# Attention over a normalised image: the exchange of flipped blocks sent through DRAM, and half of the value products in three short passes

## The reference

```python
y = group_norm(x, 4 groups) * gamma + beta           # per batch
q, k, v = split(einsum('bchw,dc->bdhw', y, w_qkv) + b_qkv)
scores = einsum('bnc,bcm->bnm', q, k) * C ** (-0.5)  # 1024 x 1024 per batch
w = softmax(scores)
a = einsum('bnm,bmc->bnc', w, v)
out = einsum('bchw,dc->bdhw', a, w_out) + b_out
return x + out
```

## Time and profile before

| | us |
|---|---|
| median of 3 runs | 137.71 (137.03 to 138.33) |
| profiled execution, device time | 138.07 |
| profiled execution, span of its instructions | 136.3 |
| PE busy | 129.4 (95%) |
| DVE busy | 99.8 (73%) |
| ACT busy | 65.0 (48%) |
| POOL busy | 41.4 (30%) |
| DMA traffic | 19.01 MB, queue q1 (SP) 53.8% of 16 engines' span |

### The profile page before, as it was taken

How to read it: one execution, slowest core, us unless ns; L and a number is a source line. 1 busy time by engine, 2 the same in 40 slices (tenths; PEclk the granted TensorE clock), 3 DMA queues, 4 the chain that set the end, 5 groups by cost and what they waited for, 6 DMA issues and landing times.

```text
span 136.3 us, 1759 instructions
## 1 busy us (share of the span) xinstructions
PE 129.4 (95%) x543; PEld 89.1 (65%) x543; DVE 99.8 (73%) x170; ACT 65.0 (48%) x117; POOL 41.4 (30%) x49
## 2 busy tenths in 40 slices
PE   6999999998999949999999999999999999999990
PEld 6987688875777526666666666666656577554670
DVE  0589699999998996877686889866868886761302
ACT  3154778854675372544542475544633474730000
POOL 6032130730022229300190058000770367303210
PEclk9999999999999999999999999999999999999999
DMA  4940000030056978985689656888888459961011
GB/s 152 350 191 0 0 5 0 3 77 0 0 111 147 210 188 236 207 203 169 154 204 206 204 114 160 191 195 224 203 202 201 122 123 209 209 176 77 0 77 77
DMA packets 8937, 19.01 MB, mean 139 GB/s; under 512 B 3040, under 2 KB 3040, under 8 KB 8928
## 3 DMA queue, kind: packets, MB, share of 16 engines
q1 hardware_dynamic: 8640, 18.63, 53.8%
q10 hardware_dynamic: 288, 0.27, 0.6%
HBM read 4.20 MB, written 2.11 MB: 46 GB/s over the span
## 4 chain that ended last, share of the span: by engine, by line
PE 75%; DVE 12%; SPq 7%; issue 2%; DMA 2%; DVEq 0%
PE mixed L833 31%; PE scores L778 7%; SPq L255 7%; PE scores L779 7%; PE scores L781 7%; DVE scores L577 5%; PE scores L839 4%; PE turned L798 3%; DVE flipped_odd L605 3%; PE turned L723 3%; DMA home_odd<-flipped_odd 2%; PE mixed L830 1%; PE mixed L828 1%; PE mixed L829 1%; PE mixed L723 1%
## 5 line engine op out<-in xcount | busy, mean ns | idle before, releaser
L577 DVE TENSOR_SCALAR_CACHE_REDUCE scores<-scores,key_bias 128x1024 f32<-128x1024 f32 x31 | 40.0, 1289 | 15.0 <-PE scores L781 14.7
L426 ACT ACTIVATE probs<-scores,neg_max 128x1024 f32<-128x1024 f32 x32 | 35.7, 1116 | 22.7 <-DVE scores L577 21.9
L833 PE MATMUL mixed<-home_odd,v 128*128 128x512 f32 x48 | 22.6, 594 | 1.9 <-DMA home_odd<-flipped_odd 1.9
L833 PE MATMUL mixed<-home_even,v 128*128 128x512 f32 x48 | 22.1, 594 | 0.0
L778 PE MATMUL scores<-y_hi_odd,z_hi_odd 128*128 128x512 f32 x32 | 18.7, 585 | 0.6 <-DVE z_lo_odd L544 0.6
L778 PE MATMUL scores<-y_hi_even,z_hi_even 128*128 128x512 f32 x30 | 15.9, 531 | 0.0
L605 DVE STREAM_TRANSPOSE flipped_odd<-probs 128x1024 f32<-128x1024 f32 x12 | 14.8, 1235 | 0.3 <-DMA home_odd<-flipped_odd 0.3
L605 DVE STREAM_TRANSPOSE flipped_even<-probs 128x1024 f32<-128x1024 f32 x12 | 14.8, 1234 | 0.0
L833 PEld LDWEIGHTS mixed<-home_even,v 128*128 128x128 f32 x48 | 8.9, 189 | 7.8 <-issue 7.2
L833 PEld LDWEIGHTS mixed<-home_odd,v 128*128 128x128 f32 x48 | 8.5, 190 | 8.3 <-issue 8.0
L779 PE MATMUL scores<-y_lo_odd,z_hi_odd 128*128 128x512 f32 x32 | 12.6, 392 | 0.0
(11 more groups left out here) (162 smaller groups left out, 202.9 us busy)
## 6 DMA issues: line engine op xcount, KB each, us to landing
home_odd<-flipped_odd SPq DMA_DIRECT2D x48, 128.0 KB, 2.4
home_even<-flipped_even SPq DMA_DIRECT2D x48, 128.0 KB, 2.4
out_dram<-result SPq DMA_DIRECT2D x8, 256.0 KB, 3.5
inv_wide<-inverse_rows SPq DMA_DIRECT2D x7, 256.0 KB, 3.6
xs<-in_x_dram SPq DMA_DIRECT2D x2, 512.0 KB, 6.5
xs<-in_x_dram SPq DMA_DIRECT2D x3, 256.0 KB, 4.6
xs<-in_x_dram ACTq DMA_DIRECT2D x1, 256.0 KB, 3.3
ws<-in_weights_dram SPq DMA_DIRECT2D x1, 256.0 KB, 4.0
```

The lines of the kernel that those rows point to most:

```text
L426: act.activation(probs[:, i % RING, :], scores[:, i % 2, :], ACT.Exp, bias=neg_max[:, i:i + 1], scale=-1.0, accum_out=row_sum[:, i:i + 1]) ...
L577: dve.tensor_scalar(scores[:, i % 2, :], scores[:, i % 2, :], key_bias[:, b % 2, i:i + 1], None, ALU.subtract, ALU.min, accum_out=neg_max[ ...
L833: mm = pe.matmul(bank, v[:, b % 2, k, :], there, start=first, stop=final)
```

## The change

The sixteen DMAs from SBUF to SBUF per group become four DMAs to a DRAM buffer `squares` (`keep`, one per block, 512 KB) and eight DMAs back (`bring`, two calls of four, each DMA 256 KB to 32 partitions). `bring(g, half)` waits until both kept blocks of its half have landed. `home` has three buffers, `flipped` is a ring of four tiles. `flip(n)` now waits until the pair of blocks with n-4 has landed in DRAM. SP's order for group g is `keep(4g)`, `keep(4g+1)`, `bring(g,0)`, `keep(4g+2)`, `keep_rows(g)`, `keep(4g+3)`, `bring(g,1)`, `spread_rows(g)`, and `store(g-2)` at the end as before. `add_residual(k)` moves from POOL's slot 4k+12 to slot 4k+14.

The eight key tiles of a group are four pairs. In groups 1 to 5 pairs 2 and 3, in group 6 pairs 1, 2 and 3, 13 pairs in all, are parted: ACT copies the head (`pair_head`, 128 x 1024), POOL subtracts to get the tail in place (`pair_tail`; the very last one on DVE), and PE takes three fp32r products per tile. The product with the tail comes a slot after those with the head. For that every batch's v is split: ACT copies `v_hi` as well as `v`, POOL makes `v_lo` (`value_tail`) in each batch. In POOL's slot n, `pair_tail` comes first, then `value_tail` (slots i = 2), and `add_residual` behind them.

`y` of batches 2 and 3 is made in slots 8 and 11 (before: 9 and 17), its head in slots 9 and 14, its tail in slots 9, 10 and 14, 15. The group statistics of batches 2 and 3 go to jobs V0 and V1 of slots 5 and 6 (before: V1 and V2 of slots 6 and 8).

```diff
-            def swap(group):
-                sp.wait_ge(s_flipped, QB * group)
-                if group > 2:
-                    sp.wait_ge(s_mixed, KT * (group - 1))
-                for k in range(SQ):
-                    for g in (0, 2, 1, 3):
-                        t = g ^ k
-                        sp.dma_start(home[group % 2][32 * t:32 * t + 32, g * N:(g + 1) * N],
-                                     flipped[group % 2][32 * g:32 * g + 32, t * N:(t + 1) * N]
-                                     ).then_inc(s_swapped[group % 2], 16)
+            def keep(n):
+                group, u = n // QB, n % QB
+                sp.wait_ge(s_flipped, n - QB + 1)
+                sp.dma_start(squares[group - 1, u // 2, :, :, u % 2, :],
+                             flipped[:, n % RING, :].rearrange("p (t w) -> p t w", t=SQ)).then_inc(s_kept, 16)
+
+            def bring(group, half):
+                sp.wait_ge(s_kept, pairs_kept(QB * group + 2 * half))
+                if half == 0 and group > HOMES:
+                    sp.wait_ge(s_mixed, KT * (group - HOMES + 1))
+                for t in range(SQ):
+                    there = home[group % HOMES][32 * t:32 * t + 32, :].rearrange("p (g w) -> p g w", g=SQ)
+                    sp.dma_start(there[:, :, half * 2 * SQUARES:(half + 1) * 2 * SQUARES].bitcast(fp32),
+                                 squares[group - 1, half, :, t, :, :].rearrange("(g r) u w -> r g (u w)", g=SQ)
+                                 ).then_inc(s_swapped[group % HOMES], 16)
...
             for group in SWAPPED:
+                keep(QB * group)
+                keep(QB * group + 1)
+                bring(group, 0)
+                keep(QB * group + 2)
                 keep_rows(group)
-                swap(group)
+                keep(QB * group + 3)
+                bring(group, 1)
                 spread_rows(group)
                 if group >= 2:
                     store(group - 2)
...
+            def pair_tail(group, pair):
+                pool.wait_ge(s_head, pair_number(group, pair))
+                there = pair_at_home(group, pair)
+                pool.tensor_tensor(there, there.bitcast(fp32), pair_of_heads(pair).bitcast(fp32),
+                                   ALU.subtract).then_inc(s_parted, 1)
...
+                    if parted_in(n):
+                        pair_tail(*parted_in(n))
...
-                    if b == BATCHES - 1 and i == 2:
-                        value_tail()
+                    if n == 7:
+                        value_tail(0)
+                    elif b > 0 and i == 2:
+                        value_tail(b)
...
-                    if n >= 12 and n % QB == 0:
-                        add_residual((n - 12) // QB)
+                    if n >= 13 and n % QB == 2:
+                        add_residual((n - 14) // QB)
...
+            def pair_head(group, pair):
+                act.wait_ge(s_swapped[group % HOMES], swaps(group))
+                act.wait_ge(s_mixed, KT * (group - 1) + 2 * (pair + 1) if group > 1 else KT)
+                act.activation(pair_of_heads(pair), pair_at_home(group, pair).bitcast(fp32), ACT.Copy).then_inc(s_head, 1)
...
             def flip(n):
                 group, u = n // QB, n % QB
                 dve.wait_ge(s_exp, n + 1)
-                if group > 2:
-                    dve.wait_ge(s_swapped[group % 2], swaps(group - 2))
+                if group > SWAPPED[0]:
+                    dve.wait_ge(s_kept, pairs_kept(n - RING))
...
+                    group, turn_of_group = (n - 7) // QB, (n - 7) % QB
+                    if turn_of_group == 0:
+                        if group - 1 in SWAPPED:
+                            mix_tails(group - 1, 3)
+                        if group in SWAPPED:
+                            mix_whole(group, 0)
+                    elif group in SWAPPED:
+                        if turn_of_group == 1:
+                            mix_whole(group, 1)
+                        elif turn_of_group == 2:
+                            mix_heads(group, 2)
+                        else:
+                            mix_tails(group, 2)
+                            mix_heads(group, 3)
+            mix_heads(LAST - 1, 1)
+            mix_heads(LAST - 1, 2)
+            mix_tails(LAST - 1, 1)
+            mix_heads(LAST - 1, 3)
+            mix_tails(LAST - 1, 2)
+            mix_tails(LAST - 1, 3)
+            mix_last()
```

More of the change, by code:

```diff
@@ L43, in attention_kernel @@
     GROUP = QB * N
+    SQUARES = 32 * KT
+    HOMES = 3
     GROUPS_OF_FOUR = BATCHES * HALVES
@@ L47, in attention_kernel @@
     PAIRS = KT // 2
[L48 to L52, removed]
+    SWAP = 16 * SQ * 2
+    PARTED = {group: (2, 3) for group in SWAPPED}
+    PARTED[LAST - 1] = (1, 2, 3)
+    MIX = {4: 1, 5: 1, 6: 1, 7: 1, 8: 1, 9: 1, 10: 2}
+    squares = nc.dram_tensor("squares", (len(SWAPPED), 2, 128, SQ, 2, SQUARES), fp32)
     inverse_rows = nc.dram_tensor("inverse_rows", (GROUPS_OF_FOUR - 1, HALF), fp32)
@@ L109, in attention_kernel @@
         v = sb("v", [128, 2, KT, C])
-        v_hi, v_lo = sb("v_hi", [128, KT, C], fp32r), sb("v_lo", [128, KT, C], fp32r)
+        v_hi, v_lo = sb("v_hi", [128, 2, KT, C], fp32r), sb("v_lo", [128, 2, KT, C], fp32r)
         key_bias = sb("key_bias", [128, 2, BLOCKS])
@@ new lines, in mix_first, with mix_whole @@
+            def mix_first(tiles):
+                for k in tiles:
+                    if k == 0:
+                        mix_waits(0)
+                    if k % QB == 0:
+                        pe.wait_ge(s_copied[k // QB], QB)
+                    pe.matmul(mixed[:, 0, :], v[:, 0, k, :], first_turned[:, k, :], start=k == 0,
+                              stop=k == KT - 1).then_inc(s_mixed, 1)
+            def mix_whole(group, pair):
+                b, g = group // HALVES, group % HALVES
+                if pair == 0:
+                    mix_waits(group)
+                for k in (2 * pair, 2 * pair + 1):
+                    pe.matmul(mixed[:, g, :], v[:, b % 2, k, :], tile_at_home(group, k).bitcast(fp32), start=k == 0,
+                              stop=False).then_inc(s_mixed, 1)
@@ new lines, in mix_heads, with mix_tails @@
+            def mix_heads(group, pair):
+                b, g = group // HALVES, group % HALVES
+                pe.wait_ge(s_v_lo, b + 1)
+                pe.wait_ge(s_head, pair_number(group, pair))
+                for k in (2 * pair, 2 * pair + 1):
+                    pe.matmul(mixed[:, g, :], v_hi[:, b % 2, k, :], tile_of_heads(k), start=False, stop=False)
+                    pe.matmul(mixed[:, g, :], v_lo[:, b % 2, k, :], tile_of_heads(k), start=False, stop=False)
+            def mix_tails(group, pair):
+                b, g = group // HALVES, group % HALVES
+                if group == LAST - 1 and pair == PAIRS - 1:
+                    pe.wait_ge(s_last_parted, 1)
+                else:
+                    pe.wait_ge(s_parted, pair_number(group, pair))
+                for k in (2 * pair, 2 * pair + 1):
+                    pe.matmul(mixed[:, g, :], v_hi[:, b % 2, k, :], tile_at_home(group, k), start=False,
+                              stop=k == KT - 1).then_inc(s_mixed, 1)
@@ new lines, in mix_last @@
+            def mix_last():
+                b, g = LAST // HALVES, LAST % HALVES
+                mix_waits(LAST)
+                for k in range(KT):
+                    if k % QB == 0:
+                        pe.wait_ge(s_copied[k // QB], turns(QB * LAST) + QB)
+                    pe.matmul(mixed[:, g, :], v_hi[:, b % 2, k, :], last_head[:, k, :], start=k == 0, stop=False)
+                    pe.matmul(mixed[:, g, :], v_hi[:, b % 2, k, :], last_tail[:, k, :], start=False, stop=False)
+                    pe.matmul(mixed[:, g, :], v_lo[:, b % 2, k, :], last_head[:, k, :], start=False,
+                              stop=k == KT - 1).then_inc(s_mixed, 1)
```

164 lines of the change are left out of this document (95 added, 69 removed).

## The result

| | us |
|---|---|
| kernel with the change, median of 4 runs | 185.42 (185.01 to 186.3) |
| kernel before, beside it | 137.84 |
| ratio, 95% interval | 1.346 (1.341 to 1.351) |
| span after / before | 183.9 / 136.3 |
| granted clock of TensorE over the span | 0.879 / 0.999 |

The change makes the kernel a third slower. The forecast had the direction, and missed the size by 36 us: 149.6, with a range of 140 to 160.

The account below looks back on a forecast made before the run. A circle over SP, DVE, ACT and POOL at 16.25 us per group was to outpace PE's 13.4: L(6) at 132.3 plus 15.9 gave span 148.2, 150.0 with 1.8 around it, stated as 149.6 us, range 140 to 160.

Parts of the forecast that it names:

- the landing of the kept blocks: Exchange to DRAM: the second keep lands 3.0 us after its issue, bounds 2.0 and 5.
- the circle over DVE, ACT and POOL: From group 3 on, SP's store waits for POOL's residual, closing a circle with PE outside: 16.25 us per group against PE's 13.4.
- Rival 1: DMA engines fill up: keeps wait behind brings and the last bring lands later; 156 us, chance 24%.
- A(3): Time SP is let go for group 3, after POOL's add_residual(0): 66.4 us.
- A(3) to A(6), three groups: SP's releases from group 3 to group 6, paced by the circle: 66.4 to 115.4 us.
- A(6) to L(6): Group 6's stores, keeps, brings and landings, from SP's release to the last bring's landing: 16.8 us, L(6) at 132.3.
- L(6) to the end of the span: Last heads, tails and value products after group 6's last bring lands: 15.9 us.
- PE's saving by parting, 4.3 us: Value products on PE: 26 tiles at 0.166 us less each, 4.3 us, 2.7 of it before slot 28.
- rival 4: Parting doesn't pay: fp32r products reading 32-word pieces run at fp32's 0.43 a pass; about 153 us, chance 5%.
- PE's loss at slot 6, 1.2 us: At the start, PE waits for DVE's spreads of the earlier group statistics: 1.2 us, of which 0.85 reaches slot 11.
- Rivals 2: Cheap circle: issues of 0.33 us and landing of 2.7 make it 15.25 us on average; 143 us, chance 18%.
- rival 3: PE stays the bound: the circle fits into 13.4 us, with a keep landed within 1.9 of A(g); 134.7 us, chance 11%.

Follow-up runs that it names:

- Experiments 11: Changed kernel with the brings of groups 4 to 6 moving only half the bytes (output not the reference's): 171.67 us, ratio 1.244.
- experiment 10: Changed kernel with all four keeps of a group issued ahead of its two brings, a semaphore for each half: 168.33 us, ratio 1.218.
- experiment 3: Changed kernel with its DRAM exchange but no parted pairs, value products of groups 1 to 6 in fp32: 187.41 us, ratio 1.364.
- experiment 6: Changed kernel with each store one group later in SP's queue, nothing else: 183.02 us, ratio 1.330.
- experiment 1: Changed kernel with each bring DMA writing the same bytes to 128 partitions instead of 32, in wrong places: 170.41 us, ratio 1.235.
- experiment 8: Changed kernel with sixteen small products of zeros on PE ahead of its wait for each group's home: 185.13 us, ratio 1.345.
- experiment 5: Old SBUF-to-SBUF exchange with the rest of the change, and each store one group later in SP's queue: 138.56 us, ratio 1.001.
- 9: As experiment 5, with POOL's last slots reordered (block 31's normalising and last batch's bias earlier, group 4's residual later): 137.28 us, ratio 0.994.
- experiments 4: Changed kernel with the old SBUF-to-SBUF exchange and two homes, the rest of the change kept: 146.61 us, no ratio given.
- experiment 2: Changed kernel with each bring's four DMAs issued in the order 0, 2, 1, 3: 181.31 us, ratio 1.321.

## Why the prediction was wrong in size

**The step that failed** is the landing of the kept blocks, taken as 3.0 us after the second keep's issue, with bounds of 2.0 and 5, and with nothing for the bring issued just before it. With idle engines a keep that follows another at once lands in 4.2 us (alone 3.2), and behind a bring, which is nearly always, in 7.2 to 8.5. Of these lines from the chain of waits of the kernel after (start us, us, what), the first is such a landing with idle engines, the others stand behind brings:

```profile
76.46 4.17 DMA squares<-flipped
83.67 7.89 DMA squares<-flipped
95.01 7.92 DMA squares<-flipped
```

The bring of 1 MB was taken with 2.7 us of moving and takes 1.05 / 210 GB/s = 5.0. The prediction treated the faster value as a choice of rate; in fact it decided how long a keep queues. Experiments 11 (less bring in front) and 10 (keeps ahead) both show it, 13.7 and 17.1 us.

**The path that it had wrong** follows from this. SP has a round of its own, through nothing but its DMAs: store and keeps, landing, bring, keep, rows and keep, landing, bring. In the prediction's own prices it takes 1.75 + 3.0 + 2.5 + 1.6 + 2.8 + 2.5 = 14.2 us, less than the 16.25 of the circle over DVE, ACT and POOL, so it never set A(g). As measured it takes 18.5, 22.0 and 22.6 us and is the longer one. The priced circle is hidden behind it: taking ACT's and POOL's part away changes nothing for the better (experiment 3), and freeing the store gives 2.4 us (experiment 6).

Rival 1 had the mechanism, at 24%, and priced it at 1.9 + 1.9 us once and 1 us per circle, 6.8 in all, where each group pays for a bring twice. Its own numbers said that a group occupies the engines for 16.1 us; that they can't be kept busy across two landings in a group was missed. Even with wide brings such a group is 18 to 21 us (experiment 1).

The sum against the trace, with A the time at which SP is let go for the store ahead of group 3 or 6, and L the landing of group 6's last bring:

| step | predicted | measured | more |
|---|---|---|---|
| A(3) | 66.4 | 75.5 | 9.1 |
| A(3) to A(6), three groups | 49.0 | 63.1 | 14.1 |
| A(6) to L(6) | 16.9 | 27.4 | 10.5 |
| L(6) to the end of the span | 15.9 | 17.9 | 2.0 |
| span | 148.2 | 183.9 | 35.7 |

Its last part can be read in the chain of waits of the kernel after (start us, us, what): group 6 goes through two landings and a bring, and then PE takes over.

```profile
139.59 8.06 DMA squares<-flipped
147.66 0.33 SPq L289
...
150.69 7.75 DMA squares<-flipped
158.46 0.30 SPq L289
...
159.75 6.25 DMA home<-squares
166.13 3.75 PE mixed L914 x4
169.89 0.43 PE mixed L922
```

Two keep landings of 8.06 and 7.75 (predicted 3.0 and 2.8) and a bring of 6.25 (2.7) are 13.6 us more than priced; cheaper issues of the brings and no gaps take 3 back. After L(6) the chain runs over PE and not, as predicted, over DVE's last tail: after its stall PE works at 1.2 GHz, so the first four products take 3.75 us instead of 1.72 and the next five 0.43 each instead of 0.23. In experiment 8, where those products run faster, the end after the last landing (167.0) is 16.6 us instead of 17.9, but that landing came 1.0 later, so the clock is worth at most 1.3 us, at the end alone.

**Point by point.**

- *PE's saving by parting, 4.3 us:* right in its price. A parted product takes 0.23 to 0.24 us, as the last group's rows do. So rival 4 is false. It was not to be had for another reason: with the old exchange 2.5 us of it are there at slot 28 (experiment 5), and nothing to 1.2 us at the end (experiments 5 and 9), where PE waits for POOL, whose tails take 2.39 (predicted 2.4).
- *PE's loss at slot 6, 1.2 us:* right. PE waits 1.1 us there for DVE's spread.
- *Head copy 1.04, pair tail 2.4:* 1.06 and 2.39. The last tail, on DVE, shows 2.18 us from 170.75; POOL's tail runs until 171.86, and POOL's residual, beside the rest of it, takes 2.29 instead of 1.28. So the 2.18 may hold a wait of one for the other, and no run has DVE's tail alone.
- *The circle through the store:* it exists, and costs 6 to 8 us with the old exchange (experiments 4 and 5). In the kernel with the change SP waits there 5.4 us ahead of group 3 and under 0.3 ahead of groups 4 to 6, and it costs 2.4 us in all (experiment 6), since SP's own round is longer. Where that round is shorter, SP stands at stores for 21.3 (experiment 1) and 47.0 us (experiment 10).
- *A(3) late by 9.1:* the two-landing rounds already run in groups 1 and 2, whose brings are issued at 35.44, 46.21, 56.97 and 67.84, 10.8 us apart. Group 1's last bring lands at 53.8 instead of 47 to 49, PE waits 3.5 us for it, and its first four products take 3.75. The prediction began the circle at group 3 and let PE set the pace until then.
- *What would show it:* DVE idle for DMAs to `squares`, ACT for DVE, PE idle before group 6's products are all there. "Groups about 16 us apart" and "SP waits for POOL from group 3 on" are wrong: they are 18.5, 22.0 and 22.6 apart, and SP's one real wait is ahead of group 3.
- *The page "SBUF — State Buffer" of the Trainium skill, section "Door 1: The DMA port swizzle":* a bring to 32 neighbouring partitions moves 210 GB/s, x into 128 partitions moved 382, and in experiment 1 a bring of the same bytes to 128 partitions moved 339 and the kernel was 15 us shorter. By the rule, narrow writes reach half of the ports, and the measurement agrees with about half (0.55 of 382, 0.62 of 339); no run shows the ports themselves.
- *Rivals 2 and 3:* rival 2 needed a landing of 2.7 us, rival 3 a keep issued and landed within 1.9. None landed under 3.2.

**Not tried:** brings that fill the right place in 128 partitions, which the layout of `squares` would have to allow, half of the exchange on another engine's queue, and experiment 10 with the stores a group later or with wide brings, so that nothing shows how far the gains add up. Where the 4 us of experiment 2 come from is open as well.

## What to carry to other kernels

How long a transfer takes to land depends on what stands before it in the DMA engines as much as on its size (here 3.2 to 8.5 us for the same 512 KB): for each DMA on a circle of waits, add the moving time of everything that is issued ahead of it and still under way, at the rate of its own form, and count how many landings are waited for in a round. Price every circle that closes, the shortest too: one that looks hidden can become the longest when one of its terms is wrong. And where work moves off the bound engine, look at the last two groups on the engine that takes it: here most of the gain was gone there.

## What the runs showed of the hardware

- DMAs from DRAM to 32 partitions moved 210 GB/s at full share, to 128 partitions 339 (experiment 1, share 0.97); DMAs from 128 partitions to DRAM in pieces of 1 KB moved 379, and mixed with others 347.
- Two keeps of 512 KB, issued while a bring of 1 MB is in flight, land 7.2 to 8.5 us after issue; with idle engines the first lands in 3.2 and the second in 4.2. Ordering the keeps first in the group, with the same bytes, raises the mean rate from 208 to 239 GB/s and the share from 0.79 to 0.97.
- TensorE was granted 0.85 of its clock in 60 to 150 us of the kernel after, with four products at 1.2 GHz after a stall (3.75 us against 1.72), and giving the clock back (0.94) changed the time by 0.3 us of 185, which is inside the noise.
- The order of four brings (0, 2, 1, 3 instead of 0, 1, 2, 3) was worth 3.4 to 4.1 us of 185, cause open.
- A subtraction of 128 x 1024 took 2.39 us on POOL. On DVE, with POOL's tail beside it, the same took 2.18, and POOL's next instruction 2.29 instead of 1.28.
